# Each attention of the encoder gets its own table of first ticks: nine blocks of one attention in a row at either end, alternating blocks between

## The reference

```python
x = _layernorm(x + _L0_attn_ref(x, ...))               # attention 0, with its own feed-forward inside
x = _layernorm(x + _L0_xattn_ref(x, ctx_1024, ctx_1024, ...))   # attention 1, on ctx
x = _layernorm(x + _L0_ffn_ref(x, ...))                # experts, top 2 of 8: its routing is here
# attention 0, per block of 128 tokens, 16 heads of width 8
S = einsum('bthd,buhd->btuh', q, k) - dist_scale * |t - u|     # and -inf where u < h
A = softmax(S / sqrt(8), axis=2) @ v;  x = layernorm(tokens + A @ Wo + bo)
z = layernorm(relu(x @ W1 + b1) @ W2 + b2 + x)
# attention 1, per block: keys and values from ctx, |t - u| <= 64 only
ctx = softmax(q @ k.T / sqrt(8)) @ v;  return ctx @ Wo.T + bo
# routing: logits of 8 experts per token, top 2, a place in the expert's region for each
```

## Time and profile before

| | |
|---|---|
| median of 3 runs | 1352.99 us (1351.29 to 1353.49) |
| the profiled execution | 1351.8 us, its span 1350.0 us |
| PE, PEld, DVE, ACT, POOL busy | 87%, 61%, 77%, 63%, 41% of the span |
| mean granted clock of TensorE | 0.965 |
| the encoder | from about 18 us to 665 us |
| lines L783, L1008, L793 (turn, copy, weigh) | 164.6, 154.8, 111.6 us busy |
| L971, L966 (exponentials) | 123.4, 81.7 us |
| L1136, L1169 (maximum, subtraction) | 109.7, 88.3 us |
| L720 (scatters) | 64 x 1.0 us |

### The profile page before, as it was taken

How to read it: one execution, slowest core, us unless ns; L and a number is a source line. 1 busy time by engine, 2 the same in 40 slices (tenths; PEclk the granted TensorE clock), 3 DMA queues, 4 the chain that set the end, 5 groups by cost and what they waited for, 6 DMA issues and landing times. The chain is left out here.

```text
span 1350.0 us, 31833 instructions
## 1 busy us (share of the span) xinstructions
...
## 2 busy tenths in 40 slices
PE   3789999999999999887399978999999979999796
...
GB/s 225 95 15 15 17 15 23 24 19 29 17 33 15 31 11 25 10 20 11 65 81 82 83 57 90 38 24 97 25 21 19 2 3 1 17 17 25 180 211 93
DMA packets 71490, 63.54 MB, mean 47 GB/s; under 512 B 10510, under 2 KB 61586, under 8 KB 70688
## 3 DMA queue, kind: packets, MB, share of 16 engines
...
...
## 5 line engine op out<-in xcount | busy, mean ns | idle before, releaser
L783 PE MATMUL e_bank_turned<-c_matrices,e_probs 128*128 128x128 f32 x1024 | 164.6, 285 | 19.0 <-ACT e_probs_t L1008 9.2
L709 POOL TENSOR_TENSOR e_rstd<-e_var_eps,c_minus_half 128x1 f32<-128x1 f32 x128 | 71.2, 570 | 234.6 <-DVE e_var_eps L1049 233.7
L1008 ACT ACTIVATE e_probs_t<-e_bank_turned 128x512 f32<-128x512 f32 x256 | 154.8, 605 | 14.5 <-PE e_bank_turned L783 12.9
L1136 DVE TENSOR_REDUCE e_neg_max<-e_bank_scores 128x4 f32<-128x512 f32 x160 | 109.7, 685 | 49.2 <-PE e_bank_scores L827 48.4
L783 PEld LDWEIGHTS e_bank_turned<-c_matrices,e_probs 128*128 128x128 f32 x1024 | 115.8, 144 | 43.8 <-issue 22.6
L793 PE MATMUL e_bank_mix<-e_probs_t,e_values 128*32 128x128 f32 x2048 | 111.6, 291 | 16.0 <-ACT e_probs_t L1008 15.8
L971 ACT ACTIVATE e_probs<-e_scores,e_neg_max 128x128 f32<-128x128 f32 x384 | 123.4, 411 | 1.1 <-DVE e_neg_max L1172 1.1
L1783 ACT ACTIVATE d_probs_t<-d_bank_turned 128x512 f32<-128x512 f32 x128 | 77.2, 603 | 66.1 <-PE d_bank_turned L1660 66.1
L966 ACT ACTIVATE e_probs<-e_scores 128x512 f32<-128x512 f32 x128 | 81.7, 638 | 43.0 <-DVE e_scores L1169 41.3
L712 POOL TENSOR_TENSOR e_k_by_place<-e_q_k_k,c_matrices 128x512 f32<-128x512 f32 x64 | 66.7, 1042 | 100.4 <-DVE e_q_k_k L1180 100.4
L1765 ACT ACTIVATE d_probs<-d_scores 128x512 f32<-128x512 f32 x128 | 81.0, 633 | 41.0 <-DVE d_scores L1806 39.3
...
(10 more groups left out here) (324 smaller groups left out, 3232.7 us busy)
## 6 DMA issues: line engine op xcount, KB each, us to landing
...
```

The lines of the kernel that those rows point to most:

```text
L783: last = nc.tensor.transpose(turned_bank[:, j * P:(j + 1) * P], pr[k % 3][:, j, :], c["ident"][:])
L1008: nc.scalar.activation(pt[k % 2][:], turned_bank[:], ACT.Copy).then_inc(probs_t_ready, 1)
L1136: nc.vector.tensor_reduce(nmax[k % 4][:], bank, AX.X, ALU.max, negate=True).then_inc(max_ready, 1)
```

## The change

The single table of frames is replaced by two tables of first ticks, one for each attention. Attention 0's blocks 0 to 8 begin at ticks 0, 4, ..., 32, then every 8 ticks (40, 48, ..., 216). Attention 1's blocks begin at 36, then every 8 ticks to 220, then every 4 to 252. So the 256 units take ticks 0 to 255 without an empty one (before: 0 to 287 with 32 empty). Offsets now count from the block's own first tick of that attention (`at(tick, att, offset)`); within a block they are the same as before but for these: ACT reads `x1_mix1`, `mix0_v0` and the like one tick after PE's step as before, written with `tick - 1`; `by_place` of attention 1 comes one tick later (-6 for -7); in ticks where DVE has both the joins and the row sums of attention 0, the joins (`joins`) are done at the end of the tick before; ACT takes the hidden layer ahead of the x2/x3 copy. The keys of attention 1 are projected with q1 and v1 and copied by ACT (`k1`), so DVE's op has 256 columns. xT and ctxT get rings and loads of their own (4 each). Rings: x_bo 4 to 6, x_ln2b 5 to 9, x2 2 to 6, x3 10 to 16, values 3 to 4, row numbers 2 to 3, q_k 6 to 3; scatter semaphores 8 to 12. The table's two scratch tiles lie in the scores' memory, so DVE waits for all probabilities ahead of the table. The bias constant of attention 0 has 12 heads in place of 16 (the first four come by L813).

```diff
-SHIFT = 4
 FRAME = 2 * G
-
-
-def at(tick, offset, count=BATCH):
-
-    n, rest = divmod(tick - offset, FRAME)
-    return n if rest == 0 and 0 <= n < count else None
+DENSE = 8
+FIRST0 = [G * n + G * max(n - DENSE, 0) for n in range(BATCH)]
+FIRST1 = [G * (DENSE + 1) + FRAME * n - G * max(n - (BATCH - 1 - DENSE), 0) for n in range(BATCH)]
+BATCH_AT = {first: n for n, first in enumerate(FIRST0)}, {first: n for n, first in enumerate(FIRST1)}
+
+
+def at(tick, att, offset):
+
+    return BATCH_AT[att].get(tick - offset)
 
 
...
 def group_at(tick, offset):
 
-    n = at(tick, offset)
-    ends = [GROUP_FIRST[i] + GROUP_SIZE[i] - 1 for i in range(GROUPS)]
-    return ends.index(n) if n in ends else None
+    n = at(tick, 1, offset)
+    return GROUP_LAST.index(n) if n in GROUP_LAST else None
 
 
 def scatter_slot(i, s):
 
-    return s if i < GROUPS - 2 else SLOTS + 2 * (i - GROUPS + 2) + s
+    return i % 2 * SLOTS + s if i < GROUPS - 2 else 2 * SLOTS + 2 * (i - GROUPS + 2) + s
 
 
 def unit_at(tick):
 
-    frame, place = divmod(tick, FRAME)
-    n = frame - SHIFT * (place // G)
-    return (place // G, n, place % G) if 0 <= n < BATCH else None
-
-
-ENCODE_TICKS = range(-8, FRAME * (BATCH + SHIFT) + 64)
+    for att in range(2):
+        for g in range(G):
+            if (n := at(tick, att, g)) is not None:
+                return att, n, g
+    return None
+
+
+ENCODE_TICKS = range(-8, FIRST1[-1] + 64)
 UNIT_NUMBER = {tick: k for k, tick in enumerate(t for t in ENCODE_TICKS if unit_at(t))}
 LIGHT = (0,)
 
 
 def light(tick):
 
-    return tick % FRAME in LIGHT
+    return unit_at(tick)[0] == 0 and unit_at(tick)[2] in LIGHT
 
 
...
+def any_at(tick, *places):
+
+    return tick if any(at(tick, *place) is not None for place in places) else None
+
+
+MIX0_V0, QK_WO1, WO0_W2, X2_X3, X1_MIX1 = (
+    ((0, 8), (0, -8)), ((0, -8), (1, 12)), ((0, 10), (0, 18)), ((1, -9), (1, 23)), ((0, 13), (1, 9)))
 VEC_TURNS = turns([("bias", 0)] + [use for tick in ENCODE_TICKS for use in (
-    ("back0", at(tick, 6)), ("qk_wo1", frame_at(tick, -8, 48)), ("wo0_w2", frame_at(tick, 10, 18)), ("back1", at(tick, 43)),
-    ("logits", group_at(tick, 61)), ("counts", group_at(tick, 69))) if use[1] is not None])
+    ("qk_wo1", any_at(tick, *QK_WO1)), ("wo0_w2", any_at(tick, *WO0_W2)), ("back0", at(tick, 0, 6)), ("back1", at(tick, 1, 7)),
+    ("logits", group_at(tick, 25)), ("counts", group_at(tick, 33))) if use[1] is not None])
 ACT_TURNS = turns([("bias", 0)] + [use for tick in ENCODE_TICKS for use in (
-    ("mix0_v0", frame_at(tick, 8, -8)), ("x2_x3", at(tick, 27, BATCH + LATE)), ("q1v1", at(tick, 28)),
-    ("x1_mix1", frame_at(tick, 13, 45)), ("hidden", at(tick, 14))) if use[1] is not None])
+    ("mix0_v0", any_at(tick, *MIX0_V0)), ("x2_x3", any_at(tick, *X2_X3)), ("q1v1", at(tick, 1, -8)),
+    ("x1_mix1", any_at(tick, *X1_MIX1)), ("hidden", at(tick, 0, 14))) if use[1] is not None])
+XT_SLOT = {tick: k % 7 for k, tick in enumerate(t for t in ENCODE_TICKS if any_at(t, *X2_X3) is not None)}
+XT_RING, X_RING, BO_RING, RES_RING, X2_RING, X3_RING, VALUES = 4, 4, 6, 9, 6, 16, 4
...
-        qkk, q1 = tiles("q_k_k", [P, 3, P], 6), tiles("q1", [P, P])
+        qk, q1, k1 = tiles("q_k", [P, 2, P], 3), tiles("q1", [P, P]), tiles("k1", [P, P])
...
-            for n in range(6):
-                load_turned(n)
-                if n < 4:
-                    load(n)
-            sp.wait_ge(vec_written, VEC_TURNS["qk_wo1", -1] + 1)
+                if n >= X_RING:
+                    sp.wait_ge(x_summed, n - X_RING + 1)
+                sp.dma_start(xin[n % X_RING][:], dram_tile(d["x"], n)).then_inc(x_loaded[n % X_RING], 16)
+
+            for n in range(X_RING):
+                load_xT(n)
+                load(n)
+            for n in range(XT_RING):
+                load_ctxT(n)
+            sp.wait_ge(vec_written, VEC_TURNS["qk_wo1", -8] + 1)
             load_experts(sp, keep, experts0, d, ("m_wgv", "m_wd", "m_bgv", "m_bd"))
             for tick in ENCODE_TICKS:
-                if (n := at(tick, -7, BATCH - 4)) is not None:
-                    load(n + 4)
-                if (n := at(tick, 29, BATCH - 6)) is not None:
-                    load_turned(n + 6)
-                if (n := at(tick, 56)) is not None:
+                if (n := at(tick, 0, -7)) is not None and n < BATCH - XT_RING:
+                    load_xT(n + XT_RING)
+                    load(n + X_RING)
+                if (n := at(tick, 1, -7)) is not None and n < BATCH - XT_RING:
+                    load_ctxT(n + XT_RING)
+                if (n := at(tick, 1, 20)) is not None:
                     sp.wait_ge(x3_ready, n + 1)
-                    sp.dma_start(dram_tile(scr["x3"], n), x3[n % 10][:]).then_inc(x3_saved[n % 10], 16)
+                    sp.dma_start(dram_tile(scr["x3"], n), x3[n % X3_RING][:]).then_inc(x3_saved[n % X3_RING], 16)
...
+                if (n := at(tick, 1, -6)) is not None:
+                    pool.wait_ge(act_read, ACT_TURNS["q1v1", n] + 1)
                     if n >= 2:
-                        pool.wait_ge(scores_done, UNIT_NUMBER[8 * n + 20] // G + 1)
+                        pool.wait_ge(scores_done, UNIT_NUMBER[FIRST1[n - 2]] // G + 1)
                     by_place(1, n)
...
                 for s in range(SLOTS):
-                    i = group_at(tick, 74 + 4 * s)
+                    i = group_at(tick, 38 + 4 * s)
                     if i is not None and i < GROUPS - 2 and s < GROUP_SIZE[i]:
                         scatter(i, s)
-                if (i := group_at(tick, 74)) is not None and i >= GROUPS - 2:
+                if (i := group_at(tick, 38)) is not None and i >= GROUPS - 2:
                     for s in range(GROUP_SIZE[i]):
                         scatter(i, s)
-                if (i := group_at(tick, 94)) is not None:
+                if (i := group_at(tick, 58)) is not None:
                     for s in range(GROUP_SIZE[i]):
-                        pool.wait_ge(r["scattered"][scatter_slot(i, s)], 32 * (i + 1 if i < GROUPS - 2 else 1))
+                        pool.wait_ge(r["scattered"][scatter_slot(i, s)], 32 * (i // 2 + 1 if i < GROUPS - 2 else 1))
                         pool.sem_inc(r["rows_free"], 1)
                     if i < GROUPS - 3:
                         pool.drain()
...
+                if (n := at(tick, 1, -8)) is not None:
                     pe.wait_ge(act_read, ACT_TURNS["q1v1", n])
-                    nc.tensor.matmul(act_bank[:, 0:P], lhsT=c["x_wq"][:], rhs=xT23[n % 7][:, 0, :], start=True, stop=True)
-                    nc.tensor.matmul(act_bank[:, P:2 * P], lhsT=xc[n % 6][:, P:2 * P], rhs=c["x_wv"][:], start=True, stop=True)\
+                    pe.wait_ge(ctxT_loaded[n % XT_RING], (n // XT_RING) * 16 + 16)
+                    nc.tensor.matmul(act_bank[:, 0:P], lhsT=c["x_wq"][:], rhs=xT23[XT_SLOT[FIRST1[n] - 9]][:, 0, :], start=True, stop=True)
+                    nc.tensor.matmul(act_bank[:, 2 * P:3 * P], lhsT=c["x_wk"][:], rhs=ctxT[n % XT_RING][:], start=True, stop=True)
+                    nc.tensor.matmul(act_bank[:, P:2 * P], lhsT=ctxT[n % XT_RING][:], rhs=c["x_wv"][:], start=True, stop=True)\
                         .then_inc(act_written, 1)
...
+                if (n := at(tick, 1, -7)) is not None:
+                    read("q1v1", n)
+                    nc.scalar.activation(q1[n % 2][:], act_bank[:, 0:P], ACT.Identity, bias=c["x_bq"][:])
+                    nc.scalar.activation(k1[n % 2][:], act_bank[:, 2 * P:3 * P], ACT.Identity, bias=c["x_bk"][:])
+                    nc.scalar.activation(va[1][n % VALUES][:, :, 0:DH], act_bank[:, P:2 * P].rearrange("p (h d) -> p h d", d=DH), ACT.Copy)\
+                        .then_inc(act_read, 1)
...
+            def joins(written):
+                read("wo0_w2", written)
+                if (n := at(written, 0, 10)) is not None:
+                    dve.wait_ge(x_summed, n + 1)
+                    last = join(sub1[n % 2][:], vec_bank[:, 0:P], x_bo[n % BO_RING][:])
+                if (n := at(written, 0, 18)) is not None:
+                    dve.wait_ge(x1_b2_ready, n + 1)
+                    last = join(sub2[n % 2][:], vec_bank[:, P:2 * P], x1_b2[n % 3][:])
+                last.then_inc(vec_read, 1)
...
+                if any_at(tick - 1, *WO0_W2) is not None and at(tick, 0, 7) is None:
+                    joins(tick - 1)
...
+                if any_at(tick, *WO0_W2) is not None and at(tick, 0, 6) is not None:
+                    joins(tick)
             dve.wait_ge(r["rows_ready"], LEAD + GROUPS)
+            dve.wait_ge(probs_ready, len(UNIT_NUMBER))
             dve_table(nc, dve, c, keep["route0"], table)
```

362 lines of the change are left out of this document (176 added, 186 removed).

## The result

The changed kernel takes 1362.46 us (median, 1361.55 to 1363.07) beside 1353.24 of the kernel before: ratio 1.007, interval 1.0055 to 1.0085. It is slower by 9.2 us, and the interval lies clear of 1, where the forecast was faster by 12.7. The profiled execution has a span of 1361.2 us against 1350.0.

The account below looks back on a forecast made before the run. PE sets the alternating frames; at the schedule's ends no engine is near full. Units -22.5, startup -0.5 and tail +10.3 sum to -12.7 us: 1339.1 profiled, 1340.3 median (forecast 1334 to 1346, full range 1328 to 1359).

Parts of the forecast that it names:

- the dense start: First nine blocks of attention 0, back to back: 84.5 us, with 9.8 us for each full block.
- the middle: 23 alternating pairs at 17.94 us plus 0.22 each for the keys' ACT copy: 417.7 us.
- the tail: Behind the last unit: 24 scatters in place of 16 on one in-order queue, +10.3 us, bounds 8 and 13.
- Blocks 1 and 2: Dense start, blocks of attention 0 with no hidden layer yet: 8.6 us each.
- the price of the ACT copy: Middle: copying attention 1's keys on ACT costs 0.22 us a frame, bounds 0 and 0.5.
- The dense attention 1: Schedule's end, nine blocks of attention 1 back to back at 9.0 us each: 84.0 us in all.
- the startup's -0.5: Startup: smaller bias and one projection fewer against two more memsets, -0.5 us, bounds -1.6 and +0.6.
- the second: Rival: each of 17 seams between dense blocks costs +1.1 us, with a late mix; +19, 1359 us; chance 0.21.
- The third: Rival: the copy in the middle costs 0.5 us a frame or more; +6.5, 1347 us; chance 0.13.
- The fourth: Rival: the dense start runs out of input as x's fifth block loads late; 1345 us if 5 late; chance 0.04.
- The first: Rival: dense ends tighter, down to occupancy, 9.1 (ACT) and 8.4 us (DVE) a block; 1329.7 us; chance 0.13.
- the line of 10.6: Sign of being wrong: blocks at the ends taking over 10.6 us on average.

Follow-up runs that it names:

- early_read: Changed kernel, but ACT reads mix0_v0 in the same tick, not one later, in ticks 28, 36, 216 and 224: ratio to before 1.0009.
- the later x2: early_read and tail_soon together on the changed kernel, with x2 turned at the end of ticks right behind a hidden layer: ratio to before 0.9964.
- best_again: Rerun: changed kernel with early_read, tail_soon, blocks 24 to 27 routed as two groups, and x2 turned later: ratio to before 0.9936.
- no_drain: Changed kernel without GpSimd's drain behind the scatters of group 5: ratio to before 1.0050.
- tail_soon: Changed kernel with groups 5 to 8 routed sooner, scatters from offset 32, no drain behind group 5: ratio to before 1.0041.
- k_back: Changed kernel with early_read, tail_soon, blocks 24 to 27 as two groups, and attention 1's keys projected as before: ratio to before 0.9906.
- k_back_x2: k_back with x2 turned later in ticks right behind a hidden layer: ratio to before 0.9893.

## Why the prediction was wrong

**Which steps failed.** The removed gaps are real, but three terms of the sum were too small: the dense start (84.5, measured 95.1), whose loop left out the turns of the shared bank; the middle (417.7, measured 428.3), whose seams to the dense ends stood at nothing; and the tail (+10.3, measured +16.4), whose queue was taken to run without waits. The first two took back nearly all of the 22.5 us, the third more than what was left.

**Where it was right.** Blocks 1 and 2 (8.6; 8.72 and 8.84), the price of the ACT copy (0.22 a pair; 0.23), and that the tail gives back more than 8 us because group 5 comes to lie behind the units. Block 0 with the clock took 9.48 for 7.5 + 1. Two hits are in part luck. The dense attention 1 (84.0, measured 82.2) holds a meeting of the shared bank at tick 224 that I had not seen; without it it takes 80.7 (early_read). And the startup's -0.5 (-0.4) can't be told: the first copy comes at 29.95 to 31.43 us in the traces of kernels with this same startup.

**The dense start: +10.5, a step that was missing.** The sum went over the loop of a dense block of attention 0 alone, and that loop was nearly right: blocks 3, 4 and 5 took 9.37, 10.05 and 10.23 us for 9.8. The next three took 15.88, 10.71 and 11.77, together 9.0 over their 29.4. From tick 25 on attention 1 is prepared in the same ticks, with x2, the projection and their reads, and I had these only in the alternating frames. I read the offsets there as costs and not as turns. In a frame of eight, -8 and 8 fall on different places; in a frame of four on the same, and the table of turns in the diff showed it. early_read and the later x2 put a number on the two meetings: block 6 goes from 15.9 to 12.4 to 10.5, 1.0 of it clock.

**The middle: +10.6, two terms.** The copy of the keys was right. The base was not: 17.94 was the mean of all 28 frames, and the first four of them (17.1 to 17.8) were light. From tick 60 to 212 the kernel before takes 18.10 a frame and the changed one 18.27 for my 18.16, +2.1 over 19 pairs. The rest are the two seams, priced at nothing: the ticks 36 to 60 took 59.1 us for three pairs of 18.16 (+4.6, 1.5 of it a stretch at half clock), the ticks 212 to 220 22.1 for one (+4.0, 1.2 of it a group's routing). With both waits mended they take 57.5 and 19.8 (best_again). The 3 us that are left at the first seam may be work of the dense blocks that is still being finished; no run shows it.

**The tail: +16.4 for +10.3.** The eight more scatters were right (24 behind 634.18), at 1.27 us each where they follow one another. Missing were the pauses between them: 2.16 and 1.56 us for the last norms of attention 1, which in the new table fall between scatters, and 2.52 for the drain, which only my bound of 13 had. I multiplied the mean distance of a queue whose longest pause was 0.61 us; the new one pauses for 6.2 in all. no_drain bears it out for the drain (the tail is 1.9 shorter); the two pauses for norms weren't taken out by themselves, and tail_soon, which removes all three, gains 4.4 since its last 16 scatters then wait for their rows.

**The sum.** Units +19.4, tail +6.1, startup +0.1 and behind the encoder -1.7, on the 1339.1 forecast for the profiled execution: 1363.0, which is its span of 1361.2 and 1.8 around it. **The rivals.** The time is near that of the second (1359), and its cause is close to it: a fixed order of shared banks over three engines. But its place was wrong: it put +1.1 on each of 17 seams between dense blocks, while these were as I had them (DVE waited 0.8 to 2.1 us for the scores at the seams of attention 1, and my loop had 1.7). The loss was in a few ticks where two attentions meet. The third didn't come true as a price (0.23 a pair and not 0.5), though the middle did cost more, by its seams. The fourth didn't occur. The first went the wrong way: no full dense block of attention 0 took 9.1 us, and those of attention 1 took 8.7 to 11.1 for its 8.4. Of the Trainium skill's two rules the one in "Perfetto Trace Analysis", section Optimization Strategy, on interleaving regimes, was the better guide: by that rule the change would lose, and it did. It was right by luck, though, since the loss came from meetings in a shared bank and from the scatters' queue. In k_back, without the long waits and the copy, the units take 588.8 us in the same dense table against 608.7 before, which speaks against it; the sooner routing wasn't tried on the old table, so how much of k_back_x2's gain is the table's stays open.

**What would have shown it wrong in the list:** the tail grew by over 13, and the first attention's dense blocks averaged 10.56, at the line of 10.6.
